# Perceiver block with a mixture-of-experts layer: the slots of the first experts' tokens are routed before the last two tiles

## What is computed

```python
logits = jnp.einsum('bsd,ed->bse', x, gate_w) + gate_b          # x: layer-normed, E = 8 experts
topv, topi = jax.lax.top_k(logits, 2)
keep = jax.nn.one_hot(topi, E, dtype=jnp.float32).sum(axis=-2)
gate_score = jax.nn.softmax(jnp.where(keep > 0, logits, -jnp.inf), axis=-1)
expert_out = jnp.einsum('bsd,edo->bseo', x, expert_w) + expert_b
out = jnp.einsum('bseo,bse->bso', expert_out, gate_score)
```

## Time and profile before

| | us |
|---|---|
| median of 3 runs | 764.32 |
| lowest and highest run | 762.08 and 765.07 |
| profiled execution, its own time | 759.4 |
| span of that execution (first to last instruction) | 757.6 |

### The profile page before, as it was taken

The page is one execution under the profiler, slowest core; times in us unless marked ns, Lnnn a source line. Parts: engine busy times, 40 slices in busy tenths (PEclk is TensorE's granted clock), DMA queues, the critical chain, the costliest instruction groups (busy, mean ns, idle before and its releaser), DMA issues. The chain is left out here.

```text
span 757.6 us, 23202 instructions
## 1 busy us (share of the span) xinstructions
PE 735.5 (97%) x9488; PEld 644.7 (85%) x9489; DVE 554.2 (73%) x1293; ACT 407.7 (54%) x930; POOL 350.3 (46%) x364
## 2 busy tenths in 40 slices
PE   8999999999999999999999999999899999599997
PEld 7899989999899998999999999997677777578884
DVE  6768796967868768687696786877889998722236
ACT  5455666565566556655566555664566664033330
POOL 0664566456455644555545745541422221246630
PEclk9999999999999999999999999999999999789999
DMA  8410301221111011010110101141862229544538
GB/s 285 153 34 26 121 3 58 65 71 59 33 34 58 11 58 53 11 61 2 58 65 2 58 9 59 57 168 57 346 268 98 118 114 363 195 136 165 183 129 326
DMA packets 23317, 78.99 MB, mean 104 GB/s; under 512 B 3344, under 2 KB 4752, under 8 KB 20144
## 3 DMA queue, kind: packets, MB, share of 16 engines
q1 hardware_dynamic: 19536, 65.50, 24.0%
q0 software_dynamic: 3680, 12.06, 4.8%
HBM read 58.93 MB, written 18.61 MB: 102 GB/s over the span
## 5 line engine op out<-in xcount | busy, mean ns | idle before, releaser
L934 DVE TENSOR_TENSOR ctx_parts_lo<-craw,ctx_parts_hi 128x1032 fp32r<-128x1032 f32 (+1 forms) x56 | 66.5, 1188 | 3.6 <-ACT ctx_parts_hi L653 3.5
L1450 PE MATMUL bank<-ctx_parts_hi,wparts 128*128 128x258 f32 x224 | 67.2, 300 | 0.0
L1452 PE MATMUL bank<-ctx_parts_lo,wparts 128*128 128x258 f32 x224 | 63.5, 283 | 0.0
L1475 PE MATMUL bank<-wparts,ctx_parts_hi 128*128 128x256 f32 x224 | 63.3, 283 | 0.0
L1451 PE MATMUL bank<-ctx_parts_hi,wparts 128*128 128x258 f32 x224 | 63.2, 282 | 0.0
L1478 PE MATMUL bank<-wparts,ctx_parts_lo 128*128 128x256 f32 x224 | 63.1, 282 | 0.0
L1477 PE MATMUL bank<-wparts,ctx_parts_hi 128*128 128x256 f32 x224 | 62.9, 281 | 0.0
L684 ACT ACTIVATE v<-bank 128x512 f32<-128x512 f32 x56 | 33.3, 594 | 54.4 <-PE bank L1478 53.7
L496 POOL TENSOR_TENSOR k_trig<-kb_even,const 128x258 f32<-128x258 f32 (+1 forms) x42 | 49.0, 1167 | 28.8 <-ACT kb_even L674 28.1
L688 ACT ACTIVATE wraw<-wraw,nmax 128x257 f32<-128x257 f32 x96 | 47.8, 501 | 22.1 <-DVE nmax L1027 21.9
L1450 PE MATMUL bank<-ctx_parts_hi,w_sums_hi 128*128 128x258 f32 x168 | 52.7, 313 | 0.0
(11 more groups left out here) (418 smaller groups left out, 2588.4 us busy)
## 6 DMA issues: line engine op xcount, KB each, us to landing
craw<-ctx_t_dram SPq DMA_DIRECT2D x32, 516.0 KB, 4.3
expert_lo<-weights_dram SPq DMA_DIRECT2D x8, 1024.0 KB, 13.1
expert_hi_scratch<-wraw SPq DMA_DIRECT2D x16, 512.0 KB, 2.6
wparts<-expert_hi_scratch SPq DMA_DIRECT2D x8, 1024.0 KB, 9.1
wraw<-weights_dram SPq DMA_DIRECT2D x5, 1024.0 KB, 5.2
expert_lo<-ffn_out_scratch SPq DMA_DIRECT2D x16, 256.0 KB, 5.4
x<-x_dram SPq DMA_DIRECT2D x8, 256.0 KB, 4.4
late_weights_raw<-weights_dram SPq DMA_DIRECT2D x2, 1024.0 KB, 5.8
```

Of the source, the lines that this page charges most:

```text
L934: dve.tensor_tensor(dst[1], src, dst[0].bitcast(F32), ALU.subtract).then_inc(s_clo, 1)
L1450: pe.matmul(psum, whi_i[:, i, cols], hi[:, i, :], start=own and i == 0, stop=False, skip_group_check=not own)
L1452: last = pe.matmul(psum, whi_i[:, i, cols], lo[:, i, :], start=False, stop=i == 1, skip_group_check=not own)
L1475: pe.matmul(psum, hi[:, i, rows], whi_i[:, i, :], start=own and u == 0 and i == 0, stop=False, skip_group_check=True)
```

## The change

Routing is done in two steps. `EARLY` is 6 tiles. From the 12 pairs per row of six tiles, the count of each expert tells how many slots its pairs already fill; the first five of these full slots (`FIRST_SLOTS`) go into a table of their own, with token and gate side by side. Pairs in them get a mark (`used_mark`) that takes them out of the second table, which has the other 18 slots (`REST`), token and gate in one pass over all 16 pair columns.

- DVE: about 20 new small steps for the full slots; the choice and flags of six tiles with tile 5's logits and top ahead of it; the residual of tile 6 goes behind that of tile 7; both layer norm variances behind the first rows. The late routing stands between `slot_lo` of slots 0 to 4.
- ACT: the one-hots of the early places, by Abs and Relu; the exponential of the early gates.
- PE: the first table behind the output product of tile 7; the transposes of slot 0 behind the last gate; late ranks behind these; second table behind the product of slot 1; the gate transposes behind the product of slot 3.
- POOL: four gathers ahead of the last two `ffn_ln`; these and later gathers wait for the stores of six tiles first and of eight from slot 5 on.
- SP: both last expert loads ahead of the stores of tiles 6 and 7. Buffers: the gather buffers lie in `craw`; output bank 6 of the last tile becomes 7.

```diff
-EARLY = TILES - 3
+EARLY = TILES - 2
+FIRST_SLOTS = EARLY - 1
+REST = SLOTS - FIRST_SLOTS
+EK = 2 * EARLY
@@ POOL
-                ffn_ln(TILES - 2)
-                ffn_ln(TILES - 1)
...
-                pool.wait_ge(s_x3d, 16 * TILES)
+                pool.wait_ge(s_x3d, 16 * EARLY)
                 pool.wait_ge(s_rows, 1)
                 for i in range(AHEAD):
                     gather(i)
+                ffn_ln(TILES - 2)
+                ffn_ln(TILES - 1)
+                gather(AHEAD)
                 pool.wait_ge(s_rows, 2)
-                for i in range(SLOTS - LATE):
+                scatter(0)
+                scatter(1)
+                pool.wait_ge(s_x3d, 16 * TILES)
+                pool.wait_ge(s_rows, 3)
+                gather(FIRST_SLOTS)
+                pool.wait_ge(s_rows, 4)
+                for i in range(2, SLOTS - LATE):
@@ ACT
+                act.wait_ge(s_rt, STEP["place"])
+                act.wait_ge(s_sc, TILES)
+                for n, (k0, k1) in enumerate(ONEHOT_PARTS):
+                    for k in range(k0, k1):
+                        last = act.activation(at_place[:, k, :], route_c[:, R_IOTA:R_IOTA + P], ACT.Abs,
+                                              bias=place[:, k:k + 1], scale=-1.0)
+                    last.then_inc(s_at_place, 1)
+                    act.wait_ge(s_at_place, 2 * n + 1)
+                    act.activation(at_place[:, k0:k1, :], at_place[:, k0:k1, :], ACT.Relu, bias=1.0,
+                                   scale=-1.0).then_inc(s_at_place, 1)
@@ DVE
-                add_out(T - 1)
+                logits_evac(T - 2)
+                top(T - 2)
...
+                choice_of(0, EARLY)
+                gap_of(0, EARLY)
...
+                first_number = b_av[:, 0:FIRST_SLOTS]
+                dve.wait_ge(s_table, 1)
...
+                dve.tensor_tensor(gather_row[:, 0:FIRST_SLOTS], first_number, first_second, ALU.add).then_inc(s_rows, 1)
...
+                ffn_ln_apply(T - 1)
+                dve.wait_ge(s_xn3, T)
@@ PE
                     for t in range(EARLY - 1):
...
+                    for t in range(EARLY):
+                        last = ranks_behind(b_q[:, NE:2 * NE], 1, 0, kept_early[:, t, :], t == 0, t == EARLY - 1)
...
+                pe.wait_ge(s_payload, 1)
+                for n, (k0, k1) in enumerate(ONEHOT_PARTS):
+                    pe.wait_ge(s_at_place, 2 * n + 2)
+                    for j in range(k0, k1):
+                        last = narrow(b_av[:, 0:2 * FIRST_SLOTS], at_place[:, j, :], first_payload[:, j, :], j == 0, j == EK - 1)
+                last.then_inc(s_table, 1)
+                pe.wait_ge(s_xo, T)
                 x3_transposed(T - 1)
...
+                pe.wait_ge(s_ewlo, HALVES)
+                slot_transposed(0, 0, 0)
+                late_ranks()
+                pe.wait_ge(s_lg, TILES)
...
+                expert_step(0, 0, 0)
+                pe.wait_ge(s_xo, T + 2)
+                expert_step(1, 1, 0)
+                late_table()
+                for i in range(2, FIRST_SLOTS - 1):
                     expert_step(i, i, 0)
-                with pe.Fori(1, LAST_ROUND) as k:
+                gates_transposed()
```

More of the change, by code:

```diff
@@ L59 @@
 K2 = 2 * TILES
-EARLY = TILES - 3
-ON_R = 10
-PAIRS = SLOTS + 1
+EARLY = TILES - 2
+FIRST_SLOTS = EARLY - 1
+REST = SLOTS - FIRST_SLOTS
+EK = 2 * EARLY
+ROUTE_STEPS = (
+    "choice", "gap", "chosen", "gate_sum", "rank_parts", "rank", "tiles_up", "rank_tile", "place", "full_flags", "full",
+    "full_before", "first_slot", "picked", "picked_sum", "past_full", "spot_open", "spot", "in_first", "gate_den", "gate_0", "gate_1",
+    "first_second", "slot_end", "slot_past", "slot_expert", "slots_left", "slots_used", "used_tiles", "used_rows",
+    "used_mark", "rank_tile_left",
+    "centred", "late_choice", "late_gap", "late_chosen", "more", "late_rank_parts", "tiles", "late_rank", "upto", "late_tiles_up",
+    "start", "late_rank_tile", "start_of_choice", "late_place", "start_tile", "whole", "late_gate_den", "late_gate_0", "late_gate_1",
+    "in_tile", "second", "spare", "late_token", "begin", "past", "expert_f", "gates_by_choice", "late_in_tile")
+STEP = {name: n + 1 for n, name in enumerate(ROUTE_STEPS)}
 HALVES = 2 * NE
@@ L142, in perceiver @@
         rstd = sbuf(top, "rstd", [P, 1])
+        with ExitStack() as same_place:
+            route_hi = sbuf(same_place, "route_hi", [P, D], F32R)
         xn = sbuf(top, "xn", [P, D])
@@ L1762, in perceiver @@
[L1762 to L1768, removed]
+            kt_flat = kt[:].rearrange("p h k -> p (h k)")
+            carved = [wraw[0][:].rearrange("p c n -> p (c n)"), wraw[1][:].rearrange("p c n -> p (c n)"), kt_flat, xn[:], qkv[2]]
@@ new lines, in perceiver @@
+            gap, gexp, gden = (carve(TILES, at=BY_XN) for _ in range(3))
+            gtop = carve(TILES, 2, at=BY_XN)
+            gates = carve(TILES, S, at=0)
+            past = carve(REST, NE - 1, at=0)
+            expert_f = carve(SLOTS, at=0)
+            slot_gate = carve(SLOTS, at=0)
+            spare, second = carve(REST, at=0), carve(REST, at=0)
+            late_token = carve(LATE, at=0)
+            late_in_tile = carve(LATE, TILES, at=0)
+            begin = carve(NE, at=0)
+            full_flags = carve(NE, EARLY, at=BY_KT)
@@ L2143, in _ @@
                     gated(i)
+                    if i == FIRST_SLOTS - 2:
+                        for j in range(2):
+                            act.wait_ge(s_gtp, j + 1)
+                            act.activation(gates_t[j], gates_bank[j][:, 0:P], ACT.Copy).then_inc(s_gt, 1)
                 act.wait_ge(s_sums, TILES)
@@ L2495, in _ @@
-                dve.wait_ge(s_rt, 22)
-                for group in place_groups[2:]:
-                    place_onehots(*group)
-                gate = gtop.rearrange("p t k -> p (t k)")
-                dve.memset(gates, 0.0)
-                dve.wait_ge(s_gexp, 1)
-                dve.tensor_scalar(gden, gexp, 1.0, None, ALU.add).then_inc(s_rt, 1)
-                dve.wait_ge(s_rt, 27)
-                dve.reciprocal(gtop[:, :, 0], gden).then_inc(s_rt, 1)
-                dve.wait_ge(s_rt, 28)
@@ new lines, in _ @@
+                dve.memset(gates, 0.0)
+                slot_lo(2, 0)
+                number = b_xt[:, 0:REST]
+                dve.wait_ge(s_table, 2)
+                dve.tensor_scalar(second, number, B * S + 0.5, -float(B * S), ALU.is_ge, ALU.mult).then_inc(s_rt, 1)
+                dve.wait_ge(s_rt, STEP["second"])
+                dve.scalar_tensor_tensor(gather_row[:, FIRST_SLOTS:SLOTS], number, 1.0, second, ALU.max, ALU.add).then_inc(s_rows, 1)
+                dve.scalar_tensor_tensor(spare, number, 0.0, rc(R_SPARE + FIRST_SLOTS, REST), ALU.is_equal, ALU.mult).then_inc(s_rt, 1)
```

365 lines of the change are left out of this document (212 added, 153 removed).

## The result

The changed kernel took **768.41 us** in the median of 5 runs (766.66 to 769.36), the kernel before 764.08 beside it (762.08 to 765.07). The ratio is 1.0055, interval [1.0039, 1.0072]: about 4.2 us slower. The profiled run took 766.66 us with a span of 764.8. Forecast were 766.9 in a range of 762.0 to 769.7, with a chance of 0.68 that the two kernels could not be told apart and of 0.25 that the change is slower by more than that.

What follows compares the result with a forecast made beforehand. Bound: when slot 0's product starts, at which clock, and how much other PE work enters the loop. +0.8 (start), +1.5 (second table) and +0.25 (gate transposes) give +2.6 us on 764.32: 766.9, range 762.0 to 769.7.

Steps and rivals of the forecast that it cites:

- The sum: Whole kernel: +0.8 us at slot 0's product, +1.5 second table, +0.25 gate transposes, together +2.6 us.
- The early part: Attention of the last tile: tile 5's early choice and more rank products start attend at about 643.5, +1.15 us.
- The first table: After ACT's output split: ACT's one-hots end last at 650.1, table stands at 650.9, first gather at 652.2, 5.5 us earlier.
- The gathers hold POOL: On POOL before the last two rstd: four gathers hold it 4.97 us, so tile 6's rstd waits until 657.3.
- POOL is not held: Rival on POOL: rstd follows the first gather at 652.8, everything after moves up 4.6 us, total 762.3; chance 0.14.
- Slot 0's product: First weight product of the slot loop on PE: starts at 664.9, 0.8 us later than before the change.
- back before slot 0's product: PE's clock: if work from 658.7 counts, full clock returns before this product, giving back 1.4 us: +1.2, so 765.5.
- low still at slot 1's: Rival on PE's clock: still 1.2 GHz at slot 1's product, which takes 4.3 not 2.9 us: +4.5, 768.8; chance 0.15.
- The second table: Inside the slot loop on PE: 128 passes of 36 columns at full clock add 1.5 us.
- Nothing else in the loop: Slot loop: no further gap, gathers 5 and 6 hidden with 1.8 us to spare; rival stall 768 to 771, chance 0.08.
- wrong ... if PE waits anywhere in the loop: Sign for the slot loop: any PE wait there, or slot 0's product starting before 662, makes the forecast wrong.

Runs made afterwards that it cites:

- The change again: The changed kernel run once more, unaltered, for a second trace; ratio to the kernel before 1.0075 [1.0055, 1.0095].
- the run that gave POOL free: Against the changed kernel, POOL computes rstd of tile 6 behind the first gather and of tile 7 behind the second, not both behind the fourth; ratio to before 1.0025.
- the load moved behind: Against the version with tile 6's variance before the first table and its rstd before the first gather: expert 7's load issued behind tile 6's store; ratio to before 1.0039.

## Why the prediction was right, point by point

**The sum.** The change again, against before, both from N: 4.01 us, of which 1.39 at slot 2, 2.06 for the table, 0.21 for the gate transposes, 0.35 in the rest of the loop and the tail. Forecast were 0.8 + 1.5 + 0.25 = 2.6. The sign, the mechanism and the place of the three terms were right; the sum was 1.4 us too small in this trace. By many runs the change costs 4.2 us in the first comparison and, at a ratio of 1.0075, 5.7 in the second, which on the forecast's base of 764.32 would be 770.1, just outside its range. So the number was right with some luck: terms sized too small, in a range wide enough for the first comparison.

**The early part: right.** Attention of the last tile +1.15 foreseen, +1.37 measured (3.98 to 5.35). ACT's split 1.15 us behind it (1.14 before), so the step is shifted whole.

**The first table: 0.7 us too early.** ACT was rightly named as the last of the three. 0.2 us are the attention's; the term that was off is the Abs: 12 took 3.5 us, 0.29 each, where 0.25 was taken from a range of 0.20 to 0.30. POOL's start behind the rows was as forecast (0.91 us). The first gather was forecast at 652.2, 13.8 us from N; measured 14.54 and 14.94.

**The gathers hold POOL: right, and it decided the outcome.** rstd was forecast 5.1 us behind the start of the first gather and came 5.0 behind (654.36 to 659.36). With this the rival "POOL is not held" is out: its price, 4.6 us, was too high as well, since the run that gave POOL free got 2.7 us at slot 0 and met the clock. For 128 rows of 2 KB the GpSimd instruction lasts 0.95 to 1.44 us here, and the computation behind it waits it out. The Trainium skill (DMA: Bandwidth & Descriptors, Anatomy of one DMA — SWDGE (gpsimd) path) calls the generation of descriptors small and says that many can be emitted before their cost shows. These rows do not agree: the cost shows with the first.

**Slot 0's product: +0.8 forecast, +1.50 measured** (25.70 to 27.20), 1.89 in the second trace. The 0.7 us of the first table are the whole miss of the first trace. The wait of PE for the kept flags at the foreseen place was 0.68. One step of the working is written short: its terms from 658.6 on add up to 662.3, not 661.8, unless the gate of tile 6 runs beside ACT's copy. It does: from the first transposes to those of slot 0 it took 3.17 us (660.63 to 663.80), 3.1 by the forecast.

**The clock.** Forecast between "back before slot 0's product" and "low still at slot 1's". It came back at 669.5, in slot 0's product, 5.7 us behind the start of slot 0's transposes as in before's trace. That agreement is chance: in the change's second trace it was 5.2 us, and 7.8 with the second table twice, a kernel whose code is the same up to there; the other seven have 5.1 to 7.8. So neither side case happened, and slot 2 is 0.3 to 0.5 us nearer to before's time than slot 0's product.

**The second table: 1.5 forecast, 2.04 measured.** It was mis-sized by 0.54 us, less than slot 0's product (0.7 and 1.1), but this part comes back in every trace. The passes themselves were right (1.60); what was missing is that the product behind 128 short instructions starts 0.44 us later, which shows in no row of before, because there a gather's wait stood behind each table. And in one execution of two came 1.3 us of gaps on top, so that the first trace has 3.42.

**Nothing else in the loop: not in the first trace.** Gathers 5 and 6 (678.24 and 679.53) delayed nobody. But PE waited 1.08 us at 715.12, and by the prediction's own sign ("wrong ... if PE waits anywhere in the loop") that spoke against it. The wait is absent from the nine other traces. The tail, from -0.4 to +1.8 us against before in the ten traces, was not in the sum.

**What no run shows** is a way to make the split pay. The best of the change's versions ended at before's end from N (119.42, the load moved behind; 119.21 before) and was 0.4% slower in the median of many runs. Take away POOL's order and the first gather's landing takes its place; take that away and the attention (1.4), the table (2.0) and the low clock remain. None of the kernels beat before by more than can be measured.

## What to carry to other kernels

Pulling a transfer forward moves it into other company: before counting the gain, look at what the queues carry at the new time (here 2 MB of weights, which made a landing of 3.6 us one of 6.0 to 6.9), and at which engine issues it and what is queued behind it there. Work that leaves a hole for a loop without gaps is paid in full, together with its price for whatever is behind it; in a hole it took time in which PE would have idled. Compare traces from a common event near the change, not from their starts: 1.4 us of the difference between these two spans arose in the first 60 us, in code that both kernels share.

## What the runs showed of the hardware that was not expected

- An indirect gather of 128 rows of 2 KB landed in 3.62 us with no plain load beside it, in 3.78 us behind two of 256 KB, and in 5.97 us behind two of 1 MB; with one of these two issued right behind the gather it was no shorter (6.46 and 6.85 us, and 6.75 for a second gather).
- Behind a row of 128 narrow products (128x36) the next product started at least 0.44 us late in all ten traces that have such a row in the loop; in two of them there were gaps of 1.3 and 2.0 us in it that the profile gives to no event.
- Fillers kept the granted clock at 2.4 GHz for as long as they ran and for some time after; it then fell to 1.2 GHz in the next hole, once 0.2 us before the work came back (661.4), and was away for 10.2 us in two traces and 3.4 in the third. In all three the return came later from N than in the same kernel without fillers (30.7 us against 29.6 and 29.7; 29.3 and 27.0 against 26.2).
- In six of the ten traces of the change and its versions the clock was low around the last tile's attention already, for 3.4 us in four of them and 6.8 us in two (its 32 products took up to 1.94 us instead of 1.08), without any hole ahead of it that the others lack. The first gather started 14.4 to 14.6 us from N in the four traces without it and 14.9 to 16.2 in the six with it.
